# Attention of a Macaron block on Trainium2: the value products of two key blocks issued together, and the output bank taken two score products later

## What is computed

```
x = x + 0.5 * ffn(layernorm(x))        # 8 experts, the best 2 per token, silu gate
x = x + attention(layernorm(x))        # the part that the change touches
x = x + 0.5 * ffn(layernorm(x))

q, k, v = split(x @ qkv_w + qkv_b)     # 16 heads of 8 channels, 4 batches
q, k = rotary(q), rotary(k)
weights = softmax(q @ k.T / sqrt(8))   # 1024 x 1024 for each of 64 (batch, head)
attention = (weights @ v) @ out_w + out_b
```

## Time and profile before

| what | value |
|---|---|
| median of 3 runs | 1265.86 us (1265.64 to 1267.74) |
| the profiled execution | 1268.65 us |
| its span, first to last instruction | 1266.9 us |
| instructions | 32082 |
| busy: PE, DVE, ACT | 1235.2, 1113.5, 799.7 us |
| PE line 981 (value), 966 (score), 933 (max) | 328.2, 321.4, 319.2 us |
| DVE line 1228, ACT line 725 | 586.0, 551.4 us |

### The profile page before, as it was taken

One profiled execution on the slowest core, in us unless ns is written; L12 is line 12 of the kernel. 1 busy time (PEld: TensorE's weight loads), 2 busy tenths in 40 slices (PEclk: granted clock), 3 DMA queues, 4 the chain that ended last, 5 costly groups with the idle time before them and its releaser, 6 DMA issues.

```text
span 1266.9 us, 32082 instructions
## 1 busy us (share of the span) xinstructions
PE 1235.2 (98%) x10208; PEld 610.7 (48%) x10208; DVE 1113.5 (88%) x2262; ACT 799.7 (63%) x1540; POOL 143.8 (11%) x450
## 2 busy tenths in 40 slices
PE   6999999999899999999999999999999999999998
PEld 4766667667522222222222222222225777767776
DVE  7889878898889999999999999999985777777775
ACT  5433333333239999999999999999995333323332
POOL 0021122201231111111111111111110000000000
PEclk9999999999959999999999999999999999999999
DMA  7000111012111111111111111111111000000000
GB/s 212 1 30 24 49 51 38 26 39 69 50 57 36 42 32 42 32 42 32 42 32 35 39 32 42 32 42 32 42 41 47 11 27 20 28 28 26 9 9 9
DMA packets 54201, 48.36 MB, mean 38 GB/s; under 512 B 11632, under 2 KB 46960, under 8 KB 54128
## 3 DMA queue, kind: packets, MB, share of 16 engines
q1 hardware_dynamic: 54128, 47.48, 12.2%
HBM read 23.73 MB, written 23.33 MB: 37 GB/s over the span
## 4 chain that ended last, share of the span: by engine, by line
PE 92%; DVE 5%; issue 1%; ACT 1%; DMA 0%; DVEq 0%; ACTq 0%
PE ps L826 25%; PE ps L981 23%; PE ps L966 22%; PE ps L813 17%; PE ps L784 1%; PE ps L803 1%; PE ps L751 1%; PE ps L933 1%; DVE mx L1228 1%; DVE X L1174 1%; PE ps L820 1%; DVE act L1162 1%; ACT probs L725 0%; PE ps L790 0%; DVE tmp L1072 0%
## 5 line engine op out<-in xcount | busy, mean ns | idle before, releaser
L1228 DVE TENSOR_REDUCE mx<-ps 128x1 f32<-128x1024 f32 x512 | 586.0, 1216 | 6.4 <-PE ps L933 2.5
L725 ACT ACTIVATE probs<-ps 128x512 f32<-128x512 f32 x1024 | 551.4, 600 | 32.2 <-PE ps L966 27.9
L654 ACT ACTIVATE sg<-ps,unscale 128x512 f32<-128x512 f32 x256 | 173.8, 687 | 281.9 <-PE ps L826 265.6
L981 PE MATMUL ps<-probs,vh 128*32 128x256 f32 x4096 | 328.2, 392 | 0.0
L966 PE MATMUL ps<-Q,K 51*128 51x512 bf16 x1024 | 321.4, 384 | 1.8 <-ACT probs L725 0.4
L933 PE MATMUL ps<-K,Q 48*128 48x512 bf16 x1008 | 319.2, 388 | 3.1 <-DVE mx L1228 2.5
L813 PEld LDWEIGHTS ps<-w,act 128*128 128x128 f32 x2048 | 248.7, 192 | 18.3 <-issue 1.4
L813 PE MATMUL ps<-w,act 128*128 128x128 f32 x2048 | 249.8, 275 | 0.0
L1162 DVE SCALAR_TENSOR_TENSOR act<-ps,unscale,sg 128x512 f32<-128x512 f32 x256 | 183.1, 745 | 56.8 <-ACT sg L654 18.1
L826 PE MATMUL ps<-x_hi,w_hi 128*128 128x512 f16 x512 | 196.0, 383 | 6.9 <-DVE act L1162 5.6
L826 PE MATMUL ps<-x_hi,w_lo 128*128 128x512 f16 x512 | 196.1, 383 | 0.0
(11 more groups left out here) (84 smaller groups left out, 597.8 us busy)
## 6 DMA issues: line engine op xcount, KB each, us to landing
o_parts<-ot SPq DMA_DIRECT2D x64, 128.0 KB, 1.9
q_stack<-parts SPq DMA_DIRECT2D x96, 64.0 KB, 2.0
k_stack<-parts SPq DMA_DIRECT2D x96, 64.0 KB, 2.0
Q<-q_stack SPq DMA_DIRECT2D x64, 96.0 KB, 2.3
K<-k_stack SPq DMA_DIRECT2D x64, 96.0 KB, 2.3
probs<-w_in SPq DMA_DIRECT2D x8, 256.0 KB, 4.9
att<-o_parts SPq DMA_DIRECT2D x16, 128.0 KB, 2.6
rden<-rdens SPq DMA_DIRECT2D x16, 128.0 KB, 2.5
```

The lines of the kernel that those rows point to most:

```text
L654: nc.scalar.activation(sg[:, j, :], hid[2 * j], ACT.Silu, scale=unscale[:, e, 2 + j:3 + j]).then_inc(silu_done, 1)
L725: nc.scalar.activation(probs[:, kb % PSLOTS, j * CH:(j + 1) * CH], score[u][i], ACT.Exp, scale=SCALE).then_inc(probs_ready, 1)
L981: last = nc.tensor.matmul(opsum[u][VW * c:VW * (c + 1), :], vh[:, u % 2, kb, :], probs[:, kb % PSLOTS, c * QW:(c + 1) * QW], start=(kb == ...
L1228: nc.vector.tensor_reduce(mx[:, u % 2, t:t + 1], pair.rearrange("p a b -> p (a b)"), AX_X, ALU.max).then_inc(max_read, 1)
```

## The change

After every second key block, behind its odd step, the value products of two blocks are issued together: behind K3 those of blocks 6 and 7 of the head before, behind K7 blocks 0 and 1, behind K11 blocks 2 and 3, behind K15 blocks 4 and 5. The bank for the output is taken at step 8 and no longer at step 6. So K6 and K7 now wait for exp 3 and exp 4, K8 takes the old output bank, K9 waits for exp 6, and V0 waits for exp 5 where it waited for exp 3. The three-bank ring, the number of instructions and their operands are the same; ACT's, DVE's, GpSimd's and SyncE's programs keep their order.

```
-LAG = 2
+BURST = 2
-OUT_AT = 6
+OUT_AT = 8
...
-                    if j == 1 and kb >= LAG:
-                        weigh_values(r, u, kb - LAG)
-                    elif j == 1 and not first:
-                        weigh_values(r + (u - 1) // QSLOTS, (u - 1) % QSLOTS, KB + kb - LAG)
+                    if j == 1 and kb % BURST == BURST - 1:
+                        for back in range(kb - 2 * BURST + 1, kb - BURST + 1):
+                            if back >= 0:
+                                weigh_values(r, u, back)
+                            elif not first:
+                                weigh_values(r + (u - 1) // QSLOTS, (u - 1) % QSLOTS, KB + back)
...
-            for kb in range(KB - LAG, KB):
+            for kb in range(KB - BURST, KB):
                 weigh_values(NH // QSLOTS - 1, QSLOTS - 1, kb)
```

## The result

The changed kernel takes 1350.66 us (median of 6 runs, 1350.47 to 1352.12), the kernel before 1265.97 beside it. The ratio is 1.0659, 95% interval 1.0646 to 1.0671: 85 us slower. The forecast was 1364 us, 1345 to 1392, and slower with 0.93.

The account below looks back on a forecast made before the run. PE's own steps bound the kernel at 9.19 us a head; four groups of 2.52 plus 0.18 and 0.49 make 10.75, 1.56 more. 1268.65 + 63 × 1.56 (98) − 2.8 = 1364 us, range 1345 to 1392.

Parts of the forecast that it names:

- PE's steps set the pace before: In the heads before, PE's own steps make 1.11 us a block, 9.19 a head with the transpose's 0.31.
- DVE is 0.15 us a head behind: DVE's reductions, 1.13 us apart, need 9.04 us a head, 0.15 less than the head takes.
- The drains that go: Four of eight changes between score and value products go: 0.19 us saved a pair, 0.76 a head.
- K3 waits for exp 0: In each group K3 needs K0's bank, so it starts 1.15 us after K0, where PE's steps give 0.66.
- K11 waits for exp 9: In K8 to K11 the transpose borrows a bank, so K11 starts at 1.64 us, not 1.15: cost 0.49.
- V0 for exp 5: Behind K7, V0 needs K5's bank and starts at 1.64 us, not 1.46: cost 0.18.
- the steps behind the fourth product: From K3 through the value products to K4: 0.31 + 3 × 0.24 + 0.34 = 1.37 us.
- What is covered: Max products' waits hide under K3's; the output's copy ends at 2.9 us, before exp 4 at 3.02.
- The signs in the profile: Profile after: exponentials idle some 100 us waiting for line 966, DVE's reductions with gaps, K3 0.05 us behind exp 0.
- Max products bind: Rival: K2's wait for DVE sets the cycle, a head about 9.5 us, about 1288 us; chance 0.05.
- The drains decide: Rival: K0 to K3 take at most 0.89 us, heads gain until DVE is full, 1257 us; chance 0.05.
- The clock falls: Rival: PE's pauses drop its clock to 1.2 GHz; a quarter of the heads so gives 1444 us; chance 0.03.

Follow-up runs that it names:

- lag_ring4_two: Kernel before with four score banks, two output banks taking turns, and DVE's reduction over half the keys: 1246.52 us, ratio 0.9837.
- burst_ring4_two: Changed kernel with four score banks, two output banks taking turns, and DVE's reduction over half the keys: 1202.27 us, ratio 0.9486.
- burst_halfmax3: Changed kernel, still three banks, with DVE's reduction over only half of the keys: 1349.26 us, ratio 1.0644.
- burst_out6: Changed kernel with the output bank taken at step 6 as before, not step 8: 1344.18 us, ratio 1.0610.
- lag_onewait: Kernel before without ACT's wait for probs_used ahead of each even exponential: 1263.17 us, ratio 0.9968.
- burst_onewait: Changed kernel without ACT's wait for probs_used ahead of each even exponential: 1340.20 us, ratio 1.0577.
- burst_ring4_lean: Changed kernel with four score banks, one output bank, DVE's reduction over half the keys, and the unread max products left out: 1212.46 us, ratio 0.9559.

## Why the prediction was right

**PE's steps set the pace before; DVE is 0.15 us a head behind.** Right. Halving DVE's work left a head of before at 9.19 us.

**The drains that go.** Expected 0.19 us for a pair of changes of shape, 0.76 a head, 48 us. Measured on four banks, where they can be had: 8.89 − 8.18 = 0.71 a head, 44 us. That the two totals are so near is luck, since two errors cancel. A group of four takes 1.98 us there and two blocks of lag_ring4_two 2.21, so a pair saves 0.23, or 0.93 a head; the difference to 0.19 lies in the steps between value products, below. The other 0.22 goes to the transpose, which this term of the prediction did not count. In the order of before it stands where the shape changes anyway and adds 0.04 us to its block. In the burst order it stands between K9 and K10, which are 0.47 apart and not 0.22. Here it is in burst_ring4_two (line 935), with K9 in front of it and K10 behind:

```profile
604.13 0.38 PE L946 MATMUL ps<-Q,K 51*128 51x512 bf16 x1
...
604.44 0.23 PE L935 MATMUL ps<-identb,mparts 128*24 128x128 bf16 x1
604.60 0.39 PE L946 MATMUL ps<-Q,K 51*128 51x512 bf16 x1
```

In the changed kernel the same 0.25 us lies under K10's wait for exp 8. The trace agrees with the rule of the Trainium skill that the prediction weighed (TensorEngine Tiling (Array Packing), Key Properties: a change of tiling mode drains the array): a score product to a value product takes 0.31 us, a value product back to a score product 0.33, where products of one kind follow each other after 0.22. It was not the rule that failed for this change, but what else the order touches.

**K3 waits for exp 0.** Expected 1.15 us from K0, measured 1.16, with 0.05 between the end of the exponential and the product. With the fourth bank this wait is gone.

**K11 waits for exp 9; V0 for exp 5.** Expected 0.49 and 0.18. K8 to K11 takes 1.64 us as counted, 0.48 more than in the other groups. V0's wait is 1.49 − 1.32 = 0.17 and goes with the bank's place.

**What was mis-sized: the steps behind the fourth product.** The prediction had 0.31 + 3 × 0.24 + 0.34 = 1.37 from K3 to K4; the trace shows 0.32 + 1.00 = 1.32. The starts of the four quarters of a burst are 0.24, 0.22 and 0.22 apart: the 0.24 that I took from the two halves of one block is paid once a burst, not at each step, and the 0.22 that I had named as the lower end, for one of the three steps, holds for two of them. With 1.16 in place of 1.15 for K3, a group is 0.04 us shorter than forecast, and with V0's wait a head is 10.58 us and not 10.75. Over the 56 heads of the loop that is 9 of the 13 us by which the forecast was high. The prediction put heads outside the loop down at the same 1.56 us. In the two profiles the three ahead of it cost 1.25 each, the three from the 61st on 2.6 us together, and the last one with all that follows is 1.8 us shorter: 6 us less in all. The profiled execution of before stood 2.8 us above its median, which gives 2.5 back.

**What is covered.** The output's copy starts 1.2 us behind V6 and leaves exp 4 just free (0.50 behind K4, as elsewhere), the max products' wait lies under K3's (burst_halfmax3), the clock stays at 1.00. All three are as expected, but for one detail: K2 stands ahead of its max product in TensorE's program and does not wait with it. It starts 0.44 behind K0, and only the max product comes at 0.61. The first head added nothing, as the prediction had assumed when it counted 63 of 64.

**The signs in the profile.** Idle time ahead of the exponentials was expected at some 100 us and is 117. DVE's reductions have gaps, 67 us. In the heads outside the loop the chain is 0.08 us shorter in each group (a head 10.34), which I had not seen ahead: ACT's separate wait is against a constant there, and an exponential starts 0.42 behind its score product.

**The rivals.** Max products bind: no, by burst_halfmax3. The drains decide: only with a fourth bank. The clock falls: not in this kernel, whose six runs have mean clocks of 0.986 and 0.987. But it fell at the end of the heads in burst_out6, lag_onewait, burst_onewait and burst_ring4_lean, which shows that the rival was not idle. The prediction held against it that the clock of before stayed at 1.00 from 955 to 960 us, 4 to 9 us behind K0 of the last head, with TensorE 91% busy. The same stretch of lag_onewait (950 to 955 us) shows the same 4.56 us busy, and there the clock falls at its end. So that row was weak ground, and what decides between the two is open.

## What to carry to other kernels

Before products of one kind are gathered, count the buffers they need in one go: with r buffers, if there are more than r of them, product r + 1 of a group waits for the whole path from the first one's start to its consumer's end, and what used to fill that time has been moved behind it. Look for the drain that a burst saves and for the buffer it runs out of in the same trace, since either alone gives the wrong sign (−44 us with four banks, +85 with three). If the order of the gains is in doubt, give the suspect one more buffer at the cost of correctness and see whether the sign turns.

## What the runs showed of the hardware that was not expected

- Between 128 × 32 products in one burst the step is 0.24 us once and 0.22 after that, for fp32 halves of 256 columns; between different key blocks nothing is added.
- One small product of another shape in the middle of a run of score products (the transpose, line 935 of burst_ring4_two) sets its neighbours 0.47 us apart in place of 0.22; between value and score products it added 0.04.
- A second wait on an instruction of ACT, against a value in a register, makes it start 0.08 us later after its score product: 0.50 with it, 0.42 without (lag_onewait). Against a constant, in the heads outside the loop, it is 0.42 with the wait in place.
- Less work made a kernel slower: burst_ring4_lean, with 504 fewer max products of 512 columns, is 10 us slower in the median than burst_ring4_two. In its profiled execution the granted clock was at half for 20 us in one place, which cost 10 us.
- The clock fell to half at the end of the heads in burst_out6, where no matmul of the 14 us ahead of it had waited longer than 0.32 us. It stayed at 1.00 at that place in the changed kernel, with much the same waits.
